# A post-norm decoder layer on one core: the first norm's products move to ScalarE, small steps are fused, and the written-out order is placed anew

## What is computed

```
x = layernorm(x + attention(x))     # causal, rotary, 32 query heads on 8 key heads of 64
x = layernorm(x + expert(x))        # two linear layers with int8 rounding of activations and weights,
                                    # weights differ by sequence: h = x q W1q, a = silu(gate)*up, a q W2q
x = layernorm(x + ffn(x))           # relu(x @ sign(up).T * up_scale) @ sign(down).T * scales, 2048 hidden
```

## Time and profile before

| | |
|---|---|
| median of 3 runs | 1388.5 us (1386.83 to 1388.78) |
| the profiled execution | 1389.54 us |
| its span, first to last instruction | 1387.5 us |
| mean granted clock of TensorE | 0.984 |
| busy share | PE 93%, DVE 73%, ACT 65%, POOL 57% |
| attention, sequences 0 and 1 | to about 549 us |
| attention of 2 and 3 with chains | to about 1090 us |
| feed-forward | to 1375 us, then the last norm and store |

### The profile page before, as it was taken

How to read it: one execution, slowest core, us unless ns; L and a number is a source line. 1 busy time by engine, 2 the same in 40 slices (tenths; PEclk the granted TensorE clock), 3 DMA queues, 4 the chain that set the end, 5 groups by cost and what they waited for, 6 DMA issues and landing times.

```text
span 1387.5 us, 25190 instructions
## 1 busy us (share of the span) xinstructions
PE 1294.3 (93%) x7112; PEld 1075.5 (78%) x7112; DVE 1012.8 (73%) x2492; ACT 904.9 (65%) x2140; POOL 784.7 (57%) x685
## 2 busy tenths in 40 slices
PE   5899999999999999989999999999998899999996
PEld 3788878888888877878877787888776676778784
DVE  3677777777677777898987888778896798875422
ACT  3676777777766776766775776677766756565332
POOL 4555565655556575646873557486661264746553
PEclk8999999999999999999999999999999999999998
DMA  4722222222222223233222222222223602100000
GB/s 138 234 62 54 61 58 63 61 69 62 73 67 54 61 55 92 85 91 85 69 69 54 69 69 55 85 54 69 58 59 121 240 15 71 56 16 31 1 31 30
DMA packets 55285, 98.78 MB, mean 71 GB/s; under 512 B 11792, under 2 KB 13840, under 8 KB 54288
## 3 DMA queue, kind: packets, MB, share of 16 engines
q1 hardware_dynamic: 55184, 97.57, 25.3%
HBM read 51.39 MB, written 4.19 MB: 40 GB/s over the span
## 4 chain that ended last, share of the span: by engine, by line
PE 75%; DVE 10%; ACT 6%; issue 5%; POOL 2%; SPq 0%; DMA 0%; ACTq 0%; DVEq 0%; POOLq 0%
PE m L1852 30%; PE ps_s L1852 9%; PE ps_o L1909 9%; PE ps_t L1897 7%; PE m L2144 7%; PE ps_t L2160 3%; PE ps_s L2160 3%; DVE pT_lo L1562 2%; PE m L1919 2%; ACT pT_hi L1276 2%; DVE o_sum L1505 1%; ACT probs L1268 1%; DVE probs L1491 1%; POOL o_lo L1094 1%; PE pc L2013 1%
## 5 line engine op out<-in xcount | busy, mean ns | idle before, releaser
L1268 ACT ACTIVATE probs<-probs,neg_max 128x128 f32<-128x128 f32 (+3 forms) x512 | 285.3, 559 | 155.7 <-DVE neg_max L1491 155.1
L1562 DVE TENSOR_TENSOR pT_lo<-ps_t,pT_hi 128x512 fp32r<-128x512 f32 (+1 forms) x384 | 220.9, 595 | 141.2 <-ACT pT_hi L1276 138.8
L1491 DVE CUSTOM_DVE_ANT_0 probs<-ps_s,mask 128x128 f32<-128x128 f32 (+3 forms) x512 | 228.3, 482 | 9.4 <-PE ps_s L1852 9.3
L1852 PE MATMUL ps_s<-k_st,q_st 128*128 128x256 f32 (+2 forms) x1024 | 231.7, 348 | 2.4 <-DMA q_st<-q_tmp 2.0
L1897 PE MATMUL ps_t<-ident,probs 128*128 128x128 f32 x1280 | 185.6, 276 | 45.5 <-DVE pT_lo L1562 35.4
L1897 PEld LDWEIGHTS ps_t<-ident,probs 128*128 128x128 f32 x1280 | 147.5, 141 | 70.3 <-DVE pT_lo L1562 44.7
L1276 ACT ACTIVATE pT_hi<-ps_t 128x512 fp32r<-128x512 f32 (+1 forms) x384 | 186.3, 519 | 13.9 <-PE ps_t L1897 10.9
L1094 POOL TENSOR_TENSOR o_lo<-o_sum,o_hi 128x512 fp32r<-128x512 f32 x64 | 81.9, 1279 | 194.1 <-ACT o_hi L1290 194.0
L1909 PE MATMUL ps_o<-pT_hi,v_st 128*128 128x256 f32 (+2 forms) x512 | 169.5, 342 | 0.0
L1909 PE MATMUL ps_o<-pT_lo,v_st 128*128 128x256 f32 (+2 forms) x512 | 156.6, 327 | 0.0
L1852 PEld LDWEIGHTS ps_s<-k_st,q_st 128*128 128x128 f32 x1024 | 151.8, 191 | 5.5 <-issue 2.6
(11 more groups left out here) (259 smaller groups left out, 3069.4 us busy)
## 6 DMA issues: line engine op xcount, KB each, us to landing
q_st<-q_tmp SPq DMA_DIRECT2D x512, 64.0 KB, 2.0
...
```

What stands on the lines that cost most here:

```text
L1268: act.activation(probs[:, h % 2, SO[i]:SO[i] + SW[i]], probs[:, h % 2, SO[i]:SO[i] + SW[i]], ACT.Exp, bias=neg_max[:, h % 2, i:i + 1], sca ...
L1491: dve.tensor_tensor_reduce(out=probs[:, h % 2, SO[i]:SO[i] + SW[i]], in0=ps_s[:, i % 2, 0:SW[i]], in1=mask[:, L - SW[i]:L], scale=-SCALE, ...
L1562: dve.tensor_tensor(pT_lo[:, d, :], ps_t[:, (h + k) % 2, 0:P * w].rearrange("p (w c) -> p w c", c=P), f32(pT_hi[:, d, :]), ALU.subtract).t ...
L1852: i = pe.matmul(dst, a, c, start=(j == 0), stop=(j == len(terms) - 1))
```

## The change

- `norm` of chain N goes from DVE to ACT: y * r + (-mean * r). POOL makes r and mean * r (`inverse_std`), ACT the negation, once for each sequence.
- `scales`, `ratio` and `variance` take immediates: one step in place of two in the first two, another form in the third.
- In `body` of PE, for b = 1: the first four of the odd product's twelve matmuls, and the whole of vT, go ahead of the third transposes.
- The last tiles: the last up tile (63) goes into m1 at once after tile 62, with hi and lo parts in free parts of xT_hi and xT_lo; down tile 61 follows, then the down tiles 62 and 63 together, bank by bank. The last sequence's rstd and power are made in two halves.
- The tables are written anew in most lines; shown are those of which the prediction speaks.

```diff
@@ ATTENTION
-    2 dve1 N0.rstd
-    3 dve1 N0.norm0
-    3 dve2 N0.norm1
-    3 pool1 N0.power
-    4 dve1 N0.norm2
-    4 dve2 N0.norm3
+    1 dve2 N0.var3 N0.rstd
+    2 pool1 N0.power
+    3 act1 N0.norm0
+    3 act2 N0.norm1
+    4 act1 N0.norm2
+    4 act2 N0.norm3
...
-    16 dve2 A0.xq1
+    17 dve1 A0.xq1
-    18 dve1 A0.wq0
-    18 dve2 A0.wq1 N1.var3
+    18 dve2 A0.wq0 A0.wq1
...
-    20 dve1 N1.norm0
-    20 dve2 N1.norm1
-    21 dve1 N1.norm2
-    21 dve2 N1.norm3
+    23 act1 N1.norm0
+    23 act2 N1.norm1
+    24 act1 N1.norm2
+    24 act2 N1.norm3
...
-    30 pe1 A1.colx
+    31 pe1 A1.colx
...
-    36 dve1 B0.xabs1
-    36 dve2 B0.xscale
+    36 dve1 B0.xabs1 B0.xscale
+    36 dve2 B0.wabs0
...
-    53 dve2 A1.xscale A1.wabs0
+    53 dve1 A1.xscale A1.wabs0
-    55 dve2 A1.xq0 A1.xq1
-    56 dve2 A1.wq0
-    57 dve1 A1.wq1
+    55 dve1 A1.xq0
+    55 dve2 A1.xq1
+    57 dve1 A1.wq0
+    57 dve2 A1.wq1
@@ FEED_FORWARD
+    66 act1 A1.wrow N2.norm0 N2.norm1 N2.norm2 N2.norm3 S7.sign S8.sign S9.sign S10.sign
+    68 pool1 N3.power
+    70 dve1 A1.prod3 N3.rstd A2.colmax0
+    72 act1 S14.sign S15.sign N3.norm0
+    74 act1 N3.norm1 N3.norm2 A2.roww N3.norm3
...
+    190 pool1 F3.add0 F3.add1 F3.add2 F3.add3 F3.power0 F3.power1
+    214 dve1 F3.var0 F3.var1 F3.rstd0 F3.var2 F3.var3 F3.rstd1 F3.norm0 F3.norm1 F3.norm2 F3.norm3
@@ build
         def tile_of(p, j):
+            ends_with = {(B - 1, PERIOD - 3): (LAST_TILE, None), (B - 1, PERIOD - 2): (None, LAST_TILE - 2),
+                         (B - 1, PERIOD - 1): (None, LAST_TILE - 1), (B, 1): (None, None)}
+            if (p, j) in ends_with:
+                return ends_with[p, j]
@@ gpsimd
+            def inverse_std(inv, mv):
+                powers[0] += 1
+                pool.tensor_tensor(inv[:, 1, :], inv[:, 0, :], half_pow[:, 1, :], ALU.pow).then_inc(powered, 1)
+                pool.wait_ge(powered, powers[0])
+                return pool.tensor_tensor(inv[:, 0, :], mv[:, :, 0], inv[:, 1, :], ALU.mult)
@@ scalar
+            def normed(n, inv, t):
+                if t == 0:
+                    negations[0] += 1
+                    act.activation(inv[:, 0, :], inv[:, 0, :], ACT.Copy, scale=-1.0).then_inc(negated, 1)
+                    act.wait_ge(negated, negations[0])
+                return act.activation(y[:, n, :], y[:, n, :], ACT.Identity, scale=inv[:, 1, t:t + 1], bias=inv[:, 0, t:t + 1])
@@ vector
             def scales(sm, j):
-                link(dve.tensor_tensor(sm[:, j, :], sm[:, j, :], bound(0, QT), ALU.max))
-                link(dve.tensor_tensor(sm[:, j, :], sm[:, j, :], bound(1, QT), ALU.mult))
+                link(dve.tensor_scalar(sm[:, j, :], sm[:, j, :], EPS, 1.0 / QMAX, ALU.max, ALU.mult))
             def ratio(sm, kt, src, inv):
-                link(dve.tensor_tensor(sm[:, 2, 0:kt], sm[:, 2, 0:kt], bound(0, kt), ALU.max))
-                return dve.tensor_tensor(sm[:, 3, 0:kt], sm[:, 2, 0:kt], inv[:, 0:kt], ALU.mult)
+                return dve.scalar_tensor_tensor(out=sm[:, 3, 0:kt], in0=sm[:, 2, 0:kt], scalar=EPS, in1=inv[:, 0:kt],
+                                                op0=ALU.max, op1=ALU.mult)
-                return dve.tensor_tensor(inv[:, 0, :], mv[:, :, 1], bound(2, QT), ALU.add)
+                return dve.tensor_scalar(inv[:, 0, d], mv[:, d, 1], LN_EPS, None, ALU.add)
@@ tensor, body
+                        if (b, h) == (1, 0) and nxt:
+                            project(m0_fill(g, b, "odd"), 0, "odd", slice(0, KT))
+                        if (b, h) == (1, 1) and nxt:
+                            project(m0_fill(g, b, "vT"), 0, "vT")
                         if half == 1:
                             later("pe2", slot(g, b, h))
                         transpose_probs(n, h, 2)
...
-                                project(m0_fill(g, b, "odd"), (b + 1) % HALF, "odd")
+                                project(m0_fill(g, b, "odd"), (b + 1) % HALF, "odd", slice(KT if b == 1 else 0, 3 * KT))
...
-                        if h == 1 and nxt:
-                            project(m0_fill(g, b, "vT"), (b + 1) % HALF, "vT")
+                        if (b, h) == (0, 1):
+                            project(m0_fill(g, b, "vT"), 1, "vT")
@@ tensor, feed
+                    tiles = (m, m + 1) if m == LAST_TILE - 1 else (m,)
                     for t in range(QT):
...
+                        for c in tiles:
+                            b, h = divmod(c, HT)
+                            if t == 0:
+                                pe.wait_ge(hid_los, c + 1)
...
```

More of the change, by code:

```diff
@@ L266 @@
+    74 dve1 B1.colmax0 B1.colmax1
+    74 pool1 B1.root A2.ws0 A2.ws1
+    75 pe1 B1.colx A2.rowsw
+    75 dve1 A2.reps B1.ratio
+    76 pe0 A2.rowsx
+    76 pe1 B1.rows
+    76 act1 B1.roww
+    76 dve1 B1.reps A2.xs0 A2.xs1
     76 pool1 B1.ws0 B1.ws1
-    77 pe1 B1.rows A2.rowsw
-    77 dve1 A2.reps B1.reps N3.norm2 N3.norm3
-    78 pe0 A2.rowsx
+    77 dve1 A2.xs2 A2.xs3 B1.xs0
     78 act1 B1.xround0
-    78 dve1 B1.xs0 B1.xs1 B1.xabs0
-    78 pool1 A2.ws0
+    78 dve1 B1.xs1 B1.xabs0
+    78 pool1 A2.ws2
@@ L334 @@
-    102 dve1 B2.ratio A3.colmax3
-    102 pool1 F0.power B2.ws0
-    103 pe0 A3.colx
-    103 pe1 B2.rows
-    103 dve1 F0.var3 B2.reps F0.rstd A3.ratio
-    104 dve1 B2.xs0 F0.norm0
-    104 pool1 B2.ws1 A3.root
-    105 dve1 F0.norm1 F0.norm2
+    97 pe0 A3.colx
+    97 dve1 A2.a0 F0.scale0 F0.scale1
+    98 dve1 F0.scale2 F0.scale3 A2.a1
+    98 pool1 F0.add2 F0.add3
+    99 dve1 F0.var0 B2.colmax0
+    100 dve1 F0.var1 B2.colmax1
+    100 pool1 A3.root B2.root
+    101 pe0 B2.colx
+    101 dve1 A3.ratio F0.var2 F0.var3
@@ L342 @@
+    102 act1 A3.roww B2.roww
+    102 dve1 B2.ratio F0.rstd
+    102 pool1 F0.power B2.ws0 A3.ws0
+    103 pe0 A3.rowsw
+    103 pe1 B2.rows A3.rowsx
+    103 dve1 A3.reps B2.reps
+    104 dve1 A3.xs0 F0.norm0 F0.norm1
+    104 pool1 B2.ws1
+    105 dve1 F0.norm2 F0.norm3
     106 act1 B2.xround0
-    106 dve1 F0.norm3 B2.xs1 B2.xabs0
+    106 dve1 B2.xs0 B2.xs1 B2.xabs0
+    106 pool1 A3.ws1
     106 sp1 F0.out
     107 dve1 B2.xabs1 B2.wabs0
-    108 act1 B2.xround1 B2.wround0 A3.roww
-    108 dve1 B2.xscale B2.wabs1 A3.reps B2.wscale
@@ new lines @@
+    127 pe1 B3.rows
+    127 dve1 B3.reps
+    128 dve1 B3.xs0 B3.xs1
+    128 pool1 F1.add0
+    129 dve1 B3.xabs0 F1.scale0 F1.scale1
+    130 act1 B3.xround0
+    130 dve1 F1.scale2 F1.scale3
+    130 pool1 F1.add1 F1.add2
+    131 dve1 B3.xabs1 F1.var0 B3.xscale
+    132 act1 B3.xround1
+    132 dve1 B3.wabs0
+    132 pool1 F1.add3
+    133 dve1 F1.var1 F1.var2
+    134 pe1 B3.xT
+    134 dve1 B3.xq
+    134 pool1 F1.power B3.ws1
+    135 dve1 F1.var3 F1.rstd
+    136 dve1 F1.norm0
+    137 dve1 F1.norm1 F1.norm2
@@ new lines @@
+    138 act1 B3.wround0 B3.wround1
+    138 dve1 F1.norm3 B3.wabs1
+    138 sp1 F1.out
+    139 dve1 B3.wscale
+    140 act1 B3.xqT B3.wqT
+    141 dve1 B3.wq
+    142 pe0 B3.wT
+    142 act1 B3.wrow
+    142 pool1 B3.add0
+    143 pe0 B3.wrow
+    143 pe1 B3.prod0
+    144 pe1 B3.prod1
+    144 dve1 B3.prod0
+    144 pool1 B3.add1 B3.add2
+    145 pe1 B3.prod2
+    145 dve1 B3.var20 B3.prod1
+    146 pe1 B3.prod3
+    146 dve1 B3.prod2 B3.var21
+    146 pool1 B3.add3
+    147 dve1 B3.prod3 B3.var22
@@ L1857, in split_terms, with project @@
                 return [(a_hi, c_hi), (a_hi, c_lo), (a_lo, c_hi)]
-            def project(fill, b_next, what):
-                wait(pe, m0_read, fill - 1)
+            def project(fill, b_next, what, part=slice(0, 3 * KT)):
+                if part.start == 0:
+                    wait(pe, m0_read, fill - 1)
                 if what == "vT":
```

448 lines of the change are left out of this document (206 added, 242 removed).

## The result

The changed kernel takes 1364.74 us (1363.76 to 1365.85) against 1388.07 (four executions of the kernel before, three of which gave the 1388.5): ratio 0.9829 [0.9817, 0.9842], 23.3 us faster, 0.8 us from the forecast of 1365.5. Its profiled execution took 1364.12 us, span 1362.3.

What follows compares the result with a forecast made beforehand. TensorE bounds both stages (busy 93% of the span), so only its waits can be won: 3.5 + 15.5 + 1.4 + 0.3 + 2.3 = 23.0 us, taking the median of 1388.5 to 1365.5 us; range 1355 to 1374.

Steps and rivals of the forecast that it cites:

- Part 1: Attention, (1, 0) and (1, 1): four odd products and vT go ahead of the third transposes; 0.35 us in ten steps, 3.5 us.
- Rival A: GpSimd's row doesn't bind and Part 1 gives its whole 1.14 us in 13 steps: 10 us more, 1355; chance 0.10.
- g = 7: Attention step where ACT and GpSimd also convert the next x and PE already waits for the softmax: gain 0.
- granted clock 1.00 from 100 to 1030 us: Sign of a right forecast: TensorE's clock stays at its full level throughout that time.
- Part 2: Attention, g = 8, 10 and 12: three long VectorE holds beside GpSimd's row go; 4.4, 5.2 and 5.9, sum 15.5 us.
- g = 11: Attention stretch with a 0.61 us wait for A1's column maxima; colx goes one slot later: 1.4 us won.
- Part 3: Norm's added work on GpSimd and ACT, four batches: cost taken as 0, at most 4 x 1.0 us without cover.
- rival C: ACT's new products lie on the path: all 16 at 0.75 would be 12 us, 1378; chance 0.05.
- Part 4: Fused small VectorE steps (scales, ratio, variance): 0.3 us, between 0 and 2; moved casts taken at 0, up to 1.3 each.
- Part 5: End of the kernel: additions start 1.87 us earlier and the first power half hides; 2.3 us, between 1.8 and 2.9.
- The signs: If right: no 3 us VectorE instruction, three stretches 14.3 to 14.8 us, (1, 1) gap about 0.6, new probs wait before (1, 2).

## Why the prediction was right, point by point

- **What TensorE waits for.** The prediction says that its waits from 100 to 500 us are of one kind. The same view has two more kinds, together 6.1 us beside the 9.1 for pT_lo:

```profile
PE ps_t L1897 <- ACT probs L1268: 3.6, 7, 1.2
PE m L1852 <- POOL o_lo L1094: 2.5, 7, 0.4
```

- **Part 1**, 3.5 us forecast over ten steps: 3.57 (2.54 + 0.19 + 0.51 + 0.33). The bound I named, the softmax before (1, 2) behind GpSimd's row, is the nearest but not the only one: with the second q_hi behind the exps, ScalarE's own queue gives the time back in (1, 2), and with it a head later SP's copies do. The number was right, the cause was half of it: the forecast named what holds this head, and not the chains that take a gain back one or two heads later. Rival A was as far off as it looked: no step got 1.14.
- **g = 7**, forecast 0: a loss of 1.8 us, from two causes. The stretch is 15.96 us in both, but I did not ask where TensorE's idle time lies. Before, gaps of 0.68, 0.76 and 1.28 us (2.72 in all); after, 1.21 and 1.98 (3.19), the clock fell behind the last, and (1, 2) takes 9.92 us in place of 8.72: 1.2 us, which the kernel with the moved products alone loses too. The other 0.53 is N0.rstd in slot 1: the forecast had a cost for casts that move beside GpSimd's work and none for this step. Both stood at 0, and these are the steps of the prediction that failed; the drop also refutes "granted clock 1.00 from 100 to 1030 us". Whether it is the place of the idle time or its amount isn't separated, and the waits alone don't settle it: with ScalarE's second q_hi in the next head, TensorE waits 1.59 us in g = 7 with b = 1 alone and 1.58 with b = 0 as well, at the same place behind the same gaps of 1.22 and 0.72; the clock fell in the first and not in the second.
- **Part 2**, 15.5 us: the three stretches won 4.48, 5.75 and 5.99 us, 16.2 in all (4.4, 5.2 and 5.9 forecast). g = 10 did better because TensorE's extra group fitted in (88 matmuls in 14.19 us, 80 in the others). g = 12 keeps only 5.07 of its 5.99: (1, 2) behind it takes 9.67 us in place of 8.77. Re-placing three names alone gives 15.2 by the medians. g = 11: 1.57 in its stretch, 1.4 forecast.
- **Part 3**, 0: holds in attention. ScalarE's 16 products, eight of them there, take 0.81 us each (0.75 forecast), and the stretch of g = 8 is 0.15 longer than an undisturbed one (0.2 forecast). That is less comfortable than it looks: the wait of over 1 us for pT_lo in slot 5, which was to show rival C, is there with 1.41 us (0.70 in g = 3). It costs next to nothing only because the wait before (1, 2) falls from 0.62 to 0.17 us. The Trainium skill's advice (page "ScalarE: Activation LUTs", section "Rules for kernel authors") to use VectorE for multiplications fits one product placed clear of the row (0.53 us against 0.81). That the move is a loss by it is not what the runs show: with N1's products on either engine g = 10 and 11 take the same.
- **Part 4**, 0.3 us: mis-sized. Alone it is worth 4.7, of which the profile has 2.1 in the third stage, where a step saved is one that can't be held beside GpSimd. The forecast counted it by VectorE's 0.16 us and not by the 1.2 that such a step takes beside GpSimd, though that stood in the bound.
- **Part 5**, 2.3 us: 2.6.
- Parts 4 and 5 together make 4.7 in "rest" where they stand alone (2.06 + 2.64); the change keeps 3.57. The other 1.1 us must be given back in the third stage's new order; TensorE waits 1.43 us there for wq, to 1134.28, and which of the re-placed pieces does it was not tried.
- **The signs.** No VectorE instruction of 3 us, the three stretches (14.34, 14.19 and 14.20), the gaps in g = 3 and the new wait came as named; the clock did not stay up, and the sign of C came without C.

That the sum comes out to 0.8 us is luck in part. It does because the loss in g = 7 and the low values of Parts 2, 4 and 5 cancel: 3.6 - 1.8 + 16.1 + 1.7 + 3.6 = 23.2, where I had 3.5 + 15.5 + 1.4 + 0.3 + 2.3 = 23.0.
